# A six-layer windowed transformer on one core: squares folded in halves and a power op for the inverse norms on GpSimd, one sine product a tile, the layer norm's affine step on ScalarE, and new orders of stages

## What is computed

```python
for i in range(6):
    x = attn_layer(shift_tokens(x), Wqkv[i], q_scale[i], k_scale[i], Wo[i]) + x
    x = ffn_layer(shift_tokens(x), ln_g[i], ln_b[i], W1[i], b1[i], W2[i], b2[i]) + x

def attn_layer(x, Wqkv, qs, ksc, Wo):        # 16 heads of 64
    q, k, v = split(x @ Wqkv)                # each b, 16, n, 64
    q = q / max(norm(q), 1e-12) * qs         # norm over the 64 of a head
    k = k / max(norm(k), 1e-12) * ksc
    q = q * cos * scale + rotate_half(q) * sin * scale
    k = k * cos / scale + rotate_half(k) * sin / scale
    ...                                      # softmax over a window of 32 + 32 keys
    return out @ Wo

def ffn_layer(x, g, bln, W1, b1, W2, b2):
    xn = (x - mean) / sqrt(var + 1e-5) * g + bln
    a, gate = split(xn @ W1 + b1)
    return a * gelu(gate) @ W2 + b2
```

## Time and profile before

| what | value |
|---|---|
| median of 3 runs | 4495.01 us (4487.22 to 4496.09) |
| span of the profiled execution | 4494.6 us |
| PE, DVE, ACT, POOL busy | 90%, 86%, 64%, 38% of the span |
| start of the stack's first unit | about 707 us |
| the 48 units' residual adds | 809.6 to 4447.3 us |
| mean granted TensorE clock | 0.976 |

### The profile page before, as it was taken

How to read it: one execution, slowest core, us unless ns; L and a number is a source line. 1 busy time by engine, 2 the same in 40 slices (tenths; PEclk the granted TensorE clock), 3 DMA queues, 4 the chain that set the end, 5 groups by cost and what they waited for, 6 DMA issues and landing times. The chain is left out here.

```text
span 4494.6 us, 104653 instructions
## 1 busy us (share of the span) xinstructions
PE 4032.1 (90%) x38560; PEld 2304.6 (51%) x38560; DVE 3861.7 (86%) x5604; ACT 2887.1 (64%) x3434; POOL 1723.6 (38%) x3226
## 2 busy tenths in 40 slices
PE   5888885999998999989999989999899999899996
PEld 2333333555555555555555555555455555555554
DVE  6888877898988999978999879898889998798985
ACT  3666663676766666666767666666666666576764
POOL 2222213444443434434444434444343434344441
PEclk8999997999999999999999999999999999999998
DMA  0000002010111111120101111110211111110102
GB/s 25 1 1 1 1 1 71 22 32 21 32 33 37 27 26 27 26 53 19 34 19 31 38 36 27 23 30 21 52 23 29 24 26 43 32 32 19 35 18 56
DMA packets 65070, 123.99 MB, mean 28 GB/s; under 512 B 15684, under 2 KB 37576, under 8 KB 64968
## 3 DMA queue, kind: packets, MB, share of 16 engines
q1 hardware_dynamic: 64968, 122.47, 11.4%
HBM read 21.99 MB, written 4.19 MB: 6 GB/s over the span
## 5 line engine op out<-in xcount | busy, mean ns | idle before, releaser
L734 POOL TENSOR_TENSOR cosq<-cosq,sinq 128x1024 f32<-128x1024 f32 x384 | 970.9, 2528 | 1665.5 <-DVE sinq L784 1665.5
L1010 PE MATMUL slot<-w_qkv,xs 128*128 128x512 f32 x2304 | 1096.5, 606 | 54.3 <-ACT xs L873 26.6
L819 DVE TENSOR_TENSOR qk<-cosq,ry 128x1024 f32<-128x1024 f32 x384 | 587.7, 1550 | 93.2 <-POOL ry L726 48.3
L1010 PEld LDWEIGHTS slot<-w_qkv,xs 128*128 128x128 f32 x2304 | 406.4, 191 | 474.4 <-issue 379.7
L784 DVE TENSOR_TENSOR sinq<-slot,table 128x512 f32<-128x512 f32 x768 | 490.6, 680 | 0.0
L781 DVE TENSOR_TENSOR cosq<-slot,table 128x1024 f32<-128x1024 f32 x384 | 467.9, 1218 | 18.8 <-ACT sq L885 6.8
L910 ACT COPY kT<-slot 64x1024 f32<-64x1024 f32 x384 | 386.6, 1007 | 120.6 <-PE slot L967 116.8
L916 ACT ACTIVATE prob<-prob 128x1024 f32<-128x1024 f32 x192 | 203.0, 1057 | 388.8 <-DVE prob L828 387.1
L803 DVE TENSOR_REDUCE ss<-sq 128x32 f32<-128x2048 f32 x192 | 437.3, 2277 | 11.3 <-ACT sq L885 11.3
L967 PEld LDWEIGHTS slot<-ident,qk 128*128 128x128 f32 x3072 | 345.1, 142 | 180.1 <-issue 92.8
L885 ACT ACTIVATE sq<-slot 128x1024 f32<-128x1024 f32 x384 | 392.5, 1022 | 66.9 <-PE slot L1010 65.6
(11 more groups left out here) (130 smaller groups left out, 6568.9 us busy)
## 6 DMA issues: line engine op xcount, KB each, us to landing
vb<-va SPq DMA_DIRECT2D x720, 130.0 KB, 2.3
w_qkv<-in_w_qkv SPq DMA_DIRECT2D x18, 512.0 KB, 4.5
w_o<-in_w_o SPq DMA_DIRECT2D x6, 512.0 KB
w<-in_w SPq DMA_DIRECT2D x6, 342.0 KB
res<-in_x SPq DMA_DIRECT2D x4, 512.0 KB, 6.2
kept<-res SPq DMA_DIRECT2D x1, 2048.0 KB, 8.7
out<-fin_res SPq DMA_DIRECT2D x8, 256.0 KB, 2.4
w<-in_w SPq DMA_DIRECT2D x6, 171.0 KB
```

Of the source, the lines that this page charges most:

```text
L734: nc.gpsimd.tensor_tensor(cosq[:, side], cosq[:, side], sinq[:, side], ALU.add).then_inc(S["qk"[side] + "_added"], 1)
L819: nc.vector.tensor_tensor(qk[:, side], cosq[:, side].rearrange("p h a d -> p h (a d)"), ry[:, side * HEADS:(side + 1) * HEADS, None].broad ...
L1010: last = nc.tensor.matmul(slot(kind, n)[:, i, :], xs[:, n * P:(n + 1) * P], w_qkv[:, "qkv".index(kind), i * SEQ:(i + 1) * SEQ], start=True ...
```

## The change

The change has five parts, all in `windowed_stack`.

1. **Squares are added in pairs first.** A new stage `fold` on POOL adds the two halves of each head's squares, 2048 values a partition to 1024, into `half_sq`. `norms` on DVE is one `reduce_sum` over the 1024, and waits for `fold`.
2. **The inverse norm by one power op.** DVE's four small instructions after the sum and POOL's twelve go. `root` on POOL is now a maximum with 1e-24 and a `pow` with -0.5, 32 values a partition each.
3. **One sine product a tile** instead of two, with a reversed pattern over the halves of the PSUM slot.
4. **The layer norm's scale and shift** go from DVE (line 854) to ACT, as a new stage `affine` in place of the tensor_scalar.
5. **New orders and slots.** All five lists and `SLOTS_OF` are written anew.

```diff
-    "o0- r1- s2- q0 kT3- va1- k0 vb1- qT3- r2- o1- s3- va2- vb2- q1 r3- k1 o2- qT0 va3- vb3- kT0 k2 o3- s0 wo- q2 "
-    "v0 mean- qT1 r0 var- v1 kT1 k3 va0 s1 h0- h1- h2- vb0 q3 v2 qT2 y- kT2 v3 ")
+    "s2- q0 kT3- va1- k0 qT3- vb1- s3- r2- q1 o1- va2- vb2- qT0 r3- k1 o2- vb3- kT0 va3- k2 o3- s0 wo- v0 q2 "
+    "mean- qT1 kT1 var- r0 k3 v1 va0 s1 h0- h1- h2- vb0 q3 qT2 kT2 v2 y- v3 o0 r1 ")
...
-    "add_k3- root3- add_q3- add_q0 root0 add_k0 add_q1 root1 add_k1 add_q2 root2 add_k2 ")
+    "root1- add_k1- fold2- add_q2- root2- add_k2- add_k3- fold3- add_q3- root3- fold0 add_q0 root0 add_k0 fold1 "
+    "add_q1 ")
...
-                if kind == "root":
-
-                    wait(pool, "seeded", unit, t)
-                    for k in range(STEPS):
-                        for i, (dst, a, b, op) in enumerate(((rt, ry, ry, ALU.mult), (rt, rt, half_ss, ALU.mult),
-                                                             (rt, rt, three_halves, ALU.add), (ry, ry, rt, ALU.mult))):
...
+                if kind == "fold":
+
+                    for name in "qk":
+                        wait(pool, name + "_squared", unit, t)
+                    wait_tile(pool, "sumsq", unit, t)
+                    squares = sq[:, :, :, :].rearrange("p a h (e d) -> p (a h) e d", e=2)
+                    nc.gpsimd.tensor_tensor(half_sq[:, :, :], squares[:, :, 0, :], squares[:, :, 1, :],
+                                            ALU.add).then_inc(S["folded"], 1)
+                elif kind == "root":
+
+                    wait(pool, "sumsq", unit, t)
+                    passed(pool)
+                    nc.gpsimd.tensor_scalar(floored[:, :], ss[:, :], 1e-24, 0.0, ALU.max, ALU.add).then_inc(S["pool_link"], 1)
+                    pool.wait_ge(S["pool_link"], unit * TPB + t + 1)
+                    for name in "qk":
+                        wait_tile(pool, name + "_scaled", unit, t)
+                    nc.gpsimd.tensor_tensor(ry[:, :], floored[:, :], minus_half[:, :], ALU.pow).then_inc(S["rooted"], 1)
...
-                for half in range(2):
-                    last = nc.vector.tensor_tensor(
-                        sinq[:, side, :, half, :], ps[:, :, 1 - half, :],
-                        sin[:, None, half * H:half * H + H].broadcast_to([P, HEADS, H]), ALU.mult)
-                last.then_inc(S[name + "_read"], 1)
+                nc.vector.tensor_tensor(
+                    sinq[:, side], ps[:, :, ::-1, :],
+                    sin.rearrange("p (a d) -> p a d", a=2)[:, None, :, :].broadcast_to([P, HEADS, 2, H]),
+                    ALU.mult).then_inc(S[name + "_read"], 1)
...
-                    nc.vector.reduce_sum(ss[:, :], sq[:, :, :, :].rearrange("p a h d -> p (a h) d"), AX.X).then_inc(S["sumsq"], 1)
...
+                    wait(dve, "folded", unit, n)
+                    wait_tile(dve, "rooted", unit, n)
+                    nc.vector.reduce_sum(ss[:, :], half_sq[:, :, :], AX.X).then_inc(S["sumsq"], 1)
...
-                    nc.vector.tensor_tensor(z[:, :], xc[:, :], sqc[:, :], ALU.mult).then_inc(S["ff_link"], 1)
-                    dve.wait_ge(S["ff_link"], 2 * unit + 2)
-                    nc.vector.tensor_scalar(z[:, :], z[:, :], vec[:, 0:1], vec[:, 1:2], ALU.mult, ALU.add).then_inc(S["z_ready"], 1)
...
+                    nc.vector.tensor_tensor(z[:, :], xc[:, :], sqc[:, :], ALU.mult).then_inc(S["normalised"], 1)
...
+                elif kind == "affine":
+                    wait(act, "normalised", unit)
+                    nc.scalar.activation(z[:, :], z[:, :], ACT.Identity, bias=vec[:, 1:2], scale=vec[:, 0:1]).then_inc(S["z_ready"], 1)
```

More of the change, by code:

```diff
@@ L889, in stage @@
                     old, unit_of = (0, unit) if n == VTILES else ((TPB - 1 if n == 0 else n), unit - 1)
-                    wait(act, "vb_filled", unit_of, old)
+                    for name in ("va", "vb"):
+                        wait(act, name + "_filled", unit_of, old)
                     wait_vb(act, unit_of, old)
@@ L1022, in stage @@
                 elif kind in ("va", "vb"):
[L1023 to L1025 removed]
+                    wait(pe, "r_read", unit, n)
+                    wait_vb(pe, unit, n)
                     passed(pe)
```

54 lines of the change are left out of this document (17 added, 37 removed), and 14 rows, old and new, of tables (DVE_ORDER, SLOTS_OF).

## The result

The changed kernel takes **5086.40 us** (median of 4 runs, 5078.17 to 5091.22) against 4495.55 for the kernel before in the same session: a ratio of 1.1313 (95% interval 1.1297 to 1.1329). It is 13% slower where 4.4% faster was forecast, and far outside the range. The profiled execution spans 5086.3 us.

What follows compares the result with a forecast made beforehand. TensorE was taken as the bound, held up by VectorE. Waits of 7.1 us a unit fall to 3.2, so 76.5 becomes 72.6: 4494.6 - 47 x (76.5 - 72.6) - 16 = 4295 us, range 4200 to 4470 (forecast's own 4220 to 4370).

Steps and rivals of the forecast that it cites:

- the layer norm's wait: TensorE's wait for the layer norm's last step: 64.8 us in all, 2.0 us a unit falling to 0.4.
- the sine: TensorE's wait for the sine product: 0.7 us a unit falling to 0.3, since VectorE gets 11 us of air.
- the copies and exp under new slots: TensorE's waits for the copy of v and exp: 2.2 us a unit falling to 1.0, slots being dealt anew.
- The sine's reversed read: VectorE's single sine product: no charge taken for reading halves reversed; half speed would add 8 x 1.2 = 10 us.
- The gates: ScalarE's table loads around exp1 delay the third gate, yet hid2 ends at 61.4 before v2 at 61.7: fits by 0.3.
- At a new layer: TensorE's wait at a layer's start: about 5.5 us stay of 8.8, saving 16 us over five layers.
- the power's price: GpSimd's power on 32 values, seen in no row: 1.2 us taken, between 0.25 and 3.9.
- the prediction's own slope: Beyond 2.3 us each us of power costs one a unit; gain used up at 6.5, 8 us gives 4565.
- the way from price to time: From power's length to kernel time: beyond 2.3 us each us delays qT0 once a unit; 3.9 us gives 4370.
- 3 us and more: Time left for the power at tiles other than tile 0 walk of the new lists.
- The rival of the lock: VectorE and GpSimd lock each other out, half the gain lost: 4370 to 4486 us, chance 0.15.
- The rival that the kernel gets slower: The power is dear and holds qT0 back; gain used up at 6.5 us, chance 0.11.

Runs made afterwards that it cites:

- mult: Multiplication of the same 32 values in place of the power, inverse norms not computed: changed kernel 4326.11 us, kernel before 4335.38 us.
- the Newton root: Changed kernel with the kernel before's inverse norm (four small VectorE instructions, three Newton steps on GpSimd) in place of the power: 4815.44 us.
- the half power: Changed kernel with the power on q's 16 values a partition only and k's multiplied: 4607.93 us.

## Why the prediction was wrong

**The total without the power came out, but not by the terms of the sum.** With mult the changed kernel takes 4326, inside the forecast's own 4220 to 4370, 31 above its middle. Part of that is luck: mult's root is 0.25 us where the sum took 1.2, and at 99 us for each microsecond that would be about 4420 (an estimate on a straight line). And the kernel before with mult, which has none of the other parts, takes 4335. So nearly all of the 4.4% came with the short root alone, while the sum gave it to the layer norm's wait, the sine, and the copies and exp under new slots. VectorE was put at 57.6 us a unit and has 57.6, ScalarE at 54.6 and has 54.5, a unit at 72.6 and has 73.9. The sine's reversed read is free, as taken; the fold was 2.36 and is 2.37. The layer norm's wait is gone with mult, as said, but for another reason: its 2.4 us on VectorE were 0.55 and an add of GpSimd, and the wait goes in the old orders too when the root is short. The prediction had seen that this row "has the length of an add in it too", and still took 2.4 for its work. The gates fit: in the run with mult the load before the third gate starts at 2452.68 and the gate at 2453.97, 1.29, with the one before it right behind the exp. Five loads against three are within 13 us of each other. The Trainium skill's 2.66 us a switch (ScalarE: Activation LUTs, "What ACT_TABLE_LOAD costs") does not show here; the rows decide. At a new layer TensorE's idle time is 6.41 to 8.45 us in that run, 7.1 on average, where 5.5 was said. Scale and shift were a little dearer, 0.82 for 0.69.

**The step that failed first is the power's price.** The prediction took 1.2 us, between 0.25 (one small instruction) and 3.9 (the twelve it replaces). Neither end was a bound: the twelve are additions and multiplications, and nothing says that a power can't cost more than what a programmer would write in its place. It takes 5.45, four and a half times the term and outside both ends. "Six and more would be 200 ns a value" was held to be unlikely; it is 158 ns a value. By the prediction's own slope this would have been small, though: with a break-even at 6.5 us, 5.45 gives 4494.6 - 47 x (6.5 - 5.45) = 4445.

**The step that failed worst is the way from price to time**, and the other 641 us are in it (31 of them the distance of 4326 to the forecast). "Beyond 2.3 us each us holds `qT0` back once a unit" asks when TensorE wants a tile's result. It does not ask who waits first. That is VectorE, which takes its list in order: at `scale` it stops, and the subtraction for exp, the residual and the rotations of the next tile stop with it. The prediction did say this of `norms` ("with `s3` and `scale_q0` queued behind it"), and not of `scale`. The two runs with shorter roots show the step failing inside the prediction's own bounds. For a root of 3.9 us it said 4370; the Newton root, 3.9 us on GpSimd, gave 4815 (with its four small instructions on VectorE back, which are 3.2 us a unit), and a power of 2.9 gave 4608. Nor are there "3 us and more" at the other tiles: at tile 3 VectorE has nothing to do between norm and scale, and waits 6.24. So the wait comes not once but four times a unit: 16.2 us. The run with the residual moved shows the queue (80 us for one row of the list), and that tile 1's wait is in part one that VectorE would have had in any case. The step from a root of 3.5 us to 5.9 shows a factor of about four, and the runs in the old orders show that it is the orders: 336 us for the same power.

**The rival of the lock was named, and stood in the wrong place.** "`scale` with a mean well above 1.7" was its sign, and 1744 ns is just past it. It was priced at 1.3 to 3.4 us a unit by the number of large GpSimd instructions. With mult the mean is 1273, lower than before in spite of the folds. What makes the lock is that one event, the root's end, releases VectorE's scale and GpSimd's next add together, so they collide every time at tiles 0 and 2. Removing that one overlap gives 272 us, 5.8 a unit. The rule of the Trainium skill (SBUF — State Buffer, "Who interferes with whom") was thus borne out: the scale, 3.30 us long in place of 1.22, gets done only once the add is over.

**The rival that the kernel gets slower** had the right mechanism and sign and the wrong threshold: 6.5 us as the point from which it decides. Between mult's 4326 and the half power's 4608, on a straight line, the new orders pass 4495 at a root of some 2.4 us, floor and link with it (an estimate, from two points).

**Where the 791 us between 5086 and 4295 went:** 31 from the forecast to the run with mult; of the power's 760, 272 for the collision of scale and add; the other 488 for waits of VectorE and what they bring. A part of both is the clock, 3.7 us a unit or 176 us by TensorE's busy time. The clock is a consequence, since the same orders with a short root run at 0.99. How much of the 488 would go if only the clock stayed high was not separated.

## What to carry to other kernels

Fewer instructions are not less time: bound an operation that the trace has never shown by a run of it alone, not by the code that it replaces. Ask of every wait, before the one who wants the result in the end, which engine reaches it first, how much that engine's list has ahead of it since the data's source, and what is queued behind; a microsecond there can count once for each time it is passed. An order tuned with one latency in it is tuned for that latency: with all other parts alike, the new lists are 100 us better than the old ones with a short root, and 323 us worse with a long one. And when a total comes out right, run the kernel before with the one change that could explain it alone: here the old kernel with a short root had the forecast's gain already.

## What the runs showed of the hardware

- GpSimd's power with two tensor operands takes 5448 ns for 32 values a partition and 2922 for 16, where its multiplication of 32 takes 253. ScalarE's Abs_reciprocal_sqrt takes 324 ns for the same 32, with a table load of 1283.
- GpSimd's adds also hold VectorE's instructions with one input: tensor_scalar of 32 values, 183 ns at the median, takes up to 2286 and then ends with the adds; in the run with three Newton steps on VectorE that line's mean is 1187. The tensor_scalar of 512 values in the layer norm takes 2461 ns at the median in the kernel before, with an add beside it, and 546 with none.
- A wait added on GpSimd made the kernel 5.3% faster (5086 to 4814), since it took away a collision that came with every second root (tiles 0 and 2).
- After an idle time of 4.94 us TensorE took 1.94 us for eight transposes that otherwise take 1.04, and the granted clock over the stack fell to 0.95.
